# A graph layer on one core: the instruction order around the change from tiles to token pairs, written anew

## The reference, cut to what matters

```python
xn  = layernorm(x)
msg = (xn @ Wr[r])[src] * weight            # one 256x256 matrix for each kind of edge
x   = x + segment_sum(msg, dst)             # graph part
    + ((q @ softmax_over_nodes(k).T @ v) * sigmoid(gate)) @ Wproj + bproj     # mixer, 8 heads
x   = x + tokens + sum over the 2 chosen of 8 experts of weight * (gelu(t @ w1 + b1) @ w2 + b2)
```

## Time and profile before

| | us |
|---|---|
| median of 3 runs | 1622.17 (1618.7 to 1623.04) |
| profiled execution | 1618.12 |
| its span, first to last instruction | 1616.2 |
| PE busy in the span | 1565.0 (97%) |
| DVE, ACT, POOL busy | 1357.8, 964.5, 1012.3 |

### The profile page before, as it was taken

The page is one execution under the profiler, slowest core; times in us unless marked ns, Lnnn a source line. Parts: engine busy times, 40 slices in busy tenths (PEclk is TensorE's granted clock), DMA queues, the critical chain, the costliest instruction groups (busy, mean ns, idle before and its releaser), DMA issues.

```text
span 1616.2 us, 31822 instructions
## 1 busy us (share of the span) xinstructions
PE 1565.0 (97%) x10509; PEld 1439.1 (89%) x10509; DVE 1357.8 (84%) x3437; ACT 964.5 (60%) x2156; POOL 1012.3 (63%) x1115
## 2 busy tenths in 40 slices
PE   7999999799999999998599999999999999999998
PEld 6888888688888888887599999999999999999998
DVE  7888766398888888885789999999999999999985
ACT  4354322255655566553467777677767776777764
POOL 4534222677777777764567777777767677777730
PEclk9999999899999999999699999999999999999999
DMA  9776665588888888888433333334333333334320
GB/s 298 261 255 250 230 240 233 181 269 288 273 282 283 284 275 283 275 282 299 127 93 112 104 118 105 112 103 121 105 106 109 108 112 102 112 105 119 105 58 10
DMA packets 127078, 290.52 MB, mean 180 GB/s; under 512 B 21271, under 2 KB 49724, under 8 KB 126914
## 3 DMA queue, kind: packets, MB, share of 16 engines
q1 hardware_dynamic: 86068, 177.19, 30.1%
q0 software_dynamic: 39952, 110.13, 25.2%
q10 hardware_dynamic: 894, 1.16, 0.2%
HBM read 149.49 MB, written 138.90 MB: 178 GB/s over the span
## 4 chain that ended last, share of the span: by engine, by line
PE 84%; DVE 5%; issue 4%; DMA 2%; ACT 2%; POOL 2%; SPq 1%; DVEq 0%; ACTq 0%; POOLq 0%
PE bank L1870 67%; PE bank L2072 4%; PE bank L2073 3%; PE bank L1916 2%; PE bank L1917 2%; PE bank L1927 1%; DVE ml L1655 1%; DMA raw<-in_L_ffn_w 1%; PE bank L2110 1%; DMA xres<-in_L_gnn_weight 1%; PE bank L2122 1%; SPq L599 1%; DVE wreg L1223 1%; DVE pad L1290 1%; PE bank L1880 1%
## 5 line engine op out<-in xcount | busy, mean ns | idle before, releaser
L853 POOL DMA_INDIRECT stg<-table,idxcur x475 | 520.0, 1095 | 230.1 <-issue 148.6
L1870 PE MATMUL bank<-wreg,xt 128*128 128x512 f32 x2352 | 582.8, 398 | 1.3 <-DVE stg L1265 1.1
L1870 PEld LDWEIGHTS bank<-wreg,xt 128*128 128x128 f32 x2352 | 436.1, 190 | 89.8 <-DVE stg L1265 1.5
L732 POOL DMA_INDIRECT raw<-table,idxa x309 | 316.0, 1023 | 91.2 <-issue 80.8
L1870 PE MATMUL bank<-tt,wreg 128*128 128x256 f32 (+1 forms) x2400 | 320.4, 283 | 0.0
L1870 PE MATMUL bank<-wreg,ht 128*128 128x256 f32 x2352 | 313.8, 282 | 0.2 <-DVE ht L1771 0.2
L1870 PEld LDWEIGHTS bank<-tt,wreg 128*128 128x128 f32 x2400 | 297.5, 190 | 2.5
L1870 PEld LDWEIGHTS bank<-wreg,ht 128*128 128x128 f32 x2352 | 292.7, 189 | 0.4 <-DVE ht L1771 0.4
L1655 DVE SCALAR_TENSOR_TENSOR ml<-stg,nrm,mh 128x256 fp32r<-128x256 f32 x483 | 207.4, 478 | 26.8 <-ACT mh L1070 26.8
L1126 ACT ACTIVATE raw<-bank,cols 128x256 f32<-128x256 f32 (+1 forms) x400 | 164.9, 463 | 98.7 <-PE bank L1870 98.7
L1070 ACT ACTIVATE mh<-stg,nrm 128x256 fp32r<-128x256 f32 x483 | 213.1, 499 | 0.5 <-DMA stg<-table,idxa 0.5
(11 more groups left out here) (246 smaller groups left out, 2122.7 us busy)
## 6 DMA issues: line engine op xcount, KB each, us to landing
table<-stg SPq DMA_DIRECT2D x196, 512.0 KB, 3.7
kv_d<-kvs SPq DMA_DIRECT2D x49, 256.5 KB, 4.5
xt_d<-xt SPq DMA_DIRECT2D x49, 256.0 KB, 4.6
xtp<-xt_d SPq DMA_DIRECT2D x24, 512.0 KB, 3.8
stg<-table,idxcur POOLq DMA_INDIRECT x475
sk<-kv_d SPq DMA_DIRECT2D x24, 256.5 KB, 5.7
out_x<-xres SPq DMA_DIRECT2D x24, 256.0 KB
xres<-in_x POOLq DMA_DIRECT2D x23, 256.0 KB, 3.8
```

The lines of the kernel that those rows point to most:

```text
L732: pool.indirect_dma_start(ring_a[:, r * EARLY + j, :], None, table[0:limit, :], bass.IndirectOffsetOnAxis(ap=idxa[:, at:at + 1], axis=0)). ...
L853: pool.indirect_dma_start(stg[:, (g % 4) * SUP + j, :], None, table, bass.IndirectOffsetOnAxis(ap=where, axis=0)).then_inc(gath[g % 4], 16)
L1870: mm = pe.matmul(dst, stat(a, c), mov(b, c), start=(n == 0), stop=(n == 3 * chunks - 1))
```

## The change

The first early entry of tile 23 (entry 0) is prepared at the start of tile 23 on ACT and DVE and no longer within tile 22. At the change of phases `spot` maps the slots of i = 0 and i = 1 to other groups: slots 0 to 3 of i = 0 do pair 0's four groups, its slots 4 to 7 the first four groups of pair 1, and the first slots of i = 1 the other four. `SLOTS_OF_FIRST` and `SLOTS_OF_SECOND` name the new order. The weight splits, the turned context and the queries move to other places; `GATES` and `OUT` of pair 0 go behind the last group of i = 0; the table of the Gelu function is loaded in slot (0, 7) by a small activation; POOL's first `roots2` goes behind all gathers of pair 1; and ACT waits for the last weight split (`w_lo`, 8) directly behind `split_hi(7)`, ahead of `NORM`, where it waited in slot (1, 4) before.

```diff
+        def spot(i, s):
+            if i == 0:
+                return (0, 2 * s + 1) if s < 4 else (1, s - 4)
+            if i == 1:
+                return (1, s + 4) if s < 4 else None
+            return (i, s) if i < NP or i == NP and s < TAIL_GROUPS else None
...
# POOL
             gathers(0, 8)
             gathers(1, 8)
+            roots2(0, 2)
...
# ACT: tile_act and the change of phases
+                if at(k, K1):
+                    early_high(k, i, b, 0)
                 if 1 in rows:
                     early_high(k, i, b, 1)
...
-                if begin or rows and nxt:
+                if rows and nxt:
                     early_high(*nxt, 0)
                 table_out(k, 4)
...
+            def expert_high(n):
+                if n == 6:
                     act.wait_ge(ctx_mm, HELD + REST)
+                split_hi(n)
+                if n == 7:
                     act.wait_ge(w_lo, 8)
+            def gelu_table():
+                act.activation(small[0:1, 156:157], small[0:1, 157:158], ACT.Gelu).then_inc(table_kept, 1)
...
+                if (i, s) == (0, 5):
+                    expert_high(4)
+                if (i, s) == (0, 6):
+                    expert_high(5)
+                if (i, s) == (0, 7):
                     query_high()
+                    gelu_table()
                     GATE_ACT(0, 2)
...
# DVE: tile_dve as tile_act, with early_prepare; the change of phases
             def WINDOW(i, s, groups):
+                for at in range(max(8 * i + s - 2, 0), 8 * i + s):
+                    done = spot(at // 8, at % 8)
+                    if done and done[1] % 2:
+                        adds(done[0], done[1] // 2)
...
+                if (i, s) == (0, 5):
                     finish_context()
+                    turned_context()
+                if (i, s) == (0, 6):
                     head_contexts()
+                    split_lo(4)
                     dve.memset(halves(c3[:]), 0.0).then_inc(c3_clear, 1)
+                if (i, s) == (0, 7):
                     query_low()
+                    split_lo(5)
...
# PE
+                if (i, s) == (0, 5):
                     context_turn()
+                if (i, s) == (0, 6):
                     context_values()
+                if (i, s) == (0, 7):
                     query_context()
                     pe.wait_ge(xtp_in, 32)
                     GATES(0, 2)
                     OUT(0, 2)
...
+SLOTS_OF_FIRST = (
+    ("*SELECT", "*MSGS", "*SUMS"),
+    ("*SELECT", "*MSGS", "*SUMS"),
+    ("*SELECT", "*WINDOW", "*MSGS", "*SUMS"),
+    ("*SELECT", "*MSGS", "*SUMS"),
+    ("*SELECT", "*WINDOW", "*MSGS", "*SUMS"),
+    ("*SELECT", "*MSGS", "*SUMS"),
+    ("*SELECT", "*WINDOW", "*MSGS", "*SUMS"),
     ("*SELECT", "*MSGS", "*SUMS"),
 )
+SLOTS_OF_SECOND = (
+    ("+GATE", "+GATE_HI", "+GATE_LOW", "+PROJ", "+EXPERT_HI 6", "*WINDOW", "+EXPERT_LOW 6"),
+    ("+STATS", "*SELECT 0", "*MSGS 0", "*SUMS 0", "+EXPERT_HI 7"),
+    ("+MEAN", "+NORM", "+EXPERT_LOW 7", "+TURN", "+TURN_HI", "+TURN_LOW", "+LAYER1 0", "+LOGIT", "*SELECT 1", "*MSGS 1",
+     "*SUMS 1"),
+    ("+LOW 0", "*SELECT 2", "*WINDOW 2", "*MSGS 2", "*SUMS 2", "+TOP", "+LAYER1 1"),
+    ("*SELECT 3", "*MSGS 3", "*SUMS 3"),
+    (),
+    ("*WINDOW 4",),
+    (),
+)
```

More of the change, by code:

```diff
@@ L53, in gps_layer @@
     SUP = 4
-    ROOTS, FIRST_ROOTS = (7, 1), (5, 0)
+    ROOTS = (7, 1)
     EARLY = 3
@@ L1133, in slot_of @@
             def slot_of(i, s, groups, p1, n1, p2, n2):
[L1134 to L1138, removed]
+                if i + s == 0:
+                    for part in PARTS_OF_SLOT[0]:
+                        exps(part)
                 in_slot(i, s, groups, p1, n1, p2, n2, MSGS=MSGS, GATE_ACT=GATE_ACT, GATE_HI=GATE_HI, NORM=NORM,
-                        TURN_HI=TURN_HI, WEIGHT=WEIGHT, COMB_HI=COMB_HI, COMBT_ACT=COMBT_ACT, LAYER1=LAYER1)
-                if isinstance(i, int) and (i, s) == (0, 7):
+                        TURN_HI=TURN_HI, WEIGHT=WEIGHT, COMB_HI=COMB_HI, COMBT_ACT=COMBT_ACT, LAYER1=LAYER1,
+                        EXPERT_HI=lambda p, nt, n: expert_high(n))
+                if i == 0 and s > 0:
+                    for part in PARTS_OF_SLOT.get(s, ()):
+                        exps(part)
+                if (i, s) == (0, 5):
[3 more added lines that the diff above has]
+                if (i, s) == (0, 7):
                     query_high()
+                    gelu_table()
                     GATE_ACT(0, 2)
-                if isinstance(i, int) and i + s > 0:
-                    beside(i, s)
             run(slot_of, NP, TAIL_GROUPS)
@@ L1646, in MSGS @@
             def MSGS(i, s, groups):
-                if s >= groups or not live(i, s):
+                if not spot(i, s):
                     return
+                i, s = spot(i, s)
                 g = group_no(i, s)
@@ L2221 @@
     ("-ADD 3", "*SELECT", "-LOW 5", "*MSGS", "+MEAN", "*WINDOW", "-LAYER1 6", "+NORM", "-LAYER2 4"),
-    ("-ADD 4", "*SELECT", "-LOW 6", "*MSGS", "*LAST_WINDOW", "-LAYER1 7", "*SUMS 4", "+TURN", "+TURN_HI", "-LAYER2 5", "*SUMS",
+    ("-ADD 4", "*SELECT", "-LOW 6", "*MSGS", "-LAYER1 7", "*SUMS 4", "+TURN", "+TURN_HI", "-LAYER2 5", "*SUMS",
      "-BIAS2"),
@@ L2227 @@
 )
-SLOTS_OF_SECOND = (
-    ("*SELECT", "*MSGS", "*WINDOW", "+GATE", "+GATE_HI", "+GATE_LOW", "*SUMS"),
-    ("*SELECT", "*MSGS", "+PROJ", "*SUMS"),
-    ("*SELECT", "*MSGS", "*WINDOW", "+STATS", "*SUMS"),
-    ("*SELECT", "*MSGS", "+MEAN", "+NORM", "*SUMS"),
-    ("*SELECT", "*WINDOW", "+TURN", "+TURN_HI", "*MSGS", "+TURN_LOW", "*SUMS"),
-    ("*SELECT", "+LAYER1 0", "+LOGIT", "*MSGS", "*LAST_WINDOW", "+LOW 0", "*SUMS"),
-    ("*SELECT", "+TOP", "*MSGS", "*WINDOW", "+LAYER1 1", "*SUMS"),
+SLOTS_OF_FIRST = (
[6 more added lines that the diff above has]
+    ("*SELECT", "*WINDOW", "*MSGS", "*SUMS"),
     ("*SELECT", "*MSGS", "*SUMS"),
 )
+SLOTS_OF_SECOND = (
[9 more added lines that the diff above has]
+)
 def in_slot(i, s, groups, p1, n1, p2, n2, **steps):
-    for entry in (SLOTS_OF_SECOND if isinstance(i, int) and i == 1 else SLOTS_OF_PAIR)[s]:
+    for entry in {0: SLOTS_OF_FIRST, 1: SLOTS_OF_SECOND}.get(i, SLOTS_OF_PAIR)[s]:
         name, *expert = entry[1:].split()
```

65 lines of the change are left out of this document (19 added, 46 removed).

## The result

The changed kernel took 1627.84 us (median of 17 runs, 1623.49 to 1634.27), the kernel before 1622.0 (17 runs, 1617.46 to 1624.63): a ratio of 1.0043, 95% interval 1.0031 to 1.0054, which is 7.0 us, 5.0 to 8.8 (the medians lie 5.8 apart). It is slower, by about what the sum gave (+7.0).

The account below looks back on a forecast made before the run. PE was taken to bound the kernel except around tile 23 and at the change of phases; -0.5 and +7.5 us gave +7.0, predicted as 1629 us against a median of 1622.17, 8-in-10 range 1620 to 1633.

Parts of the forecast that it names:

- Part two: Change of phases, from finish_context to the third expert's first layer: the legs sum to +7.5 us.
- part one: Entry 0 inside tile 23: gain at the spot at most 3.1 us, not lasting; -0.5 us taken.
- to `query_context`: Leg from finish_context: 6.46 us before, 12.5 after (+6.0), as sums, messages and a split stand in the chain.
- to `STATS`: Leg from PROJ: 7.22 us before, 3.6 after (-3.6), as two groups' messages and a split leave the gap.
- to `NORM`: Leg from STATS: 3.58 us before, 6.3 after (+2.7), as ACT waits for the last split ahead of NORM.
- to the first layer: Leg from NORM: 5.37 us before, -1.6 after, as three messages and their hand-over no longer stand between.
- to the third: Leg from first layer: 13.75 us before, +2.1 after; Gelu table gone, but sums of (1, 6) and messages come ahead.
- to finish_context: Last context part behind the sums of group (1, 0), whose gather is used 4.6 us after issue: +1.2 us.
- Rival B: The gain at tile 23 lasts as gathers land sooner: PE keeps 3.1 us, +4.4 in all; chance 0.12.
- Rival A: PE's clock comes back at the change of phases, giving back 7.3 us: -0.3 us in all; chance 0.20.
- Rival C: Weights land late beside five more gathers, so NORM comes two to four us later: +10 us; chance 0.05.
- Rival D: The change does what it says: chain steps no longer wait for messages and splits, -5 us; chance 0.08.

Follow-up runs that it names:

- tile23_only: The kernel before with part one alone: entry 0 of tile 23 prepared at the start of tile 23; ratio to before 0.9992.
- phases_only: The changed kernel with entry 0 of tile 23 put back into tile 22, so the change of phases alone; ratio to before 1.0033.
- sums6_late: The changed kernel with the sums of (1, 6) behind the second layer instead of ahead of it; ratio to before 1.0013.
- chain_first: The changed kernel with the chain's context and query steps ahead of the groups' sums, messages and split; ratio to before 1.0010.
- three_moves: The changed kernel with chain steps ahead of groups' work, the last-split wait behind the turned rows, and sums of (1, 6) behind the second layer; ratio to before 0.9965.
- warm: The changed kernel with 149 products that nobody reads added ahead of PE's waits at the change of phases; ratio to before 0.9972.
- warm_three: The kernel three_moves with 118 products that nobody reads added ahead of PE's waits; 1611.04 us, ratio to before 0.9942.

## Why the prediction was right

- **Sign and size.** +7.0 us was forecast and 1.0043, 5.0 to 8.8 us, measured. Part two alone measured 5.4 (+7.5 in the sum), part one -1.3 (interval -3.4 to +1.0; -0.5 in the sum). That the size came out so close is in part luck: from the last early entry to the third layer the traces lose some 10 us in both pairs of profiles (84.9 before and 95.1 after, 83.7 in tile23_only and 94.1 in phases_only). The forecast missed 3.3 of these at `finish_context`, and the times show 3 to 4 less than the traces.
- **The legs behind finish_context**, forecast and in the trace after: to `query_context` 12.5 and 12.49; to `PROJ` +0.7 and +0.67; to `STATS` -3.6 and -3.95; to `NORM` +2.7 and +2.40; to the first layer -1.6 and -1.71; to the third +2.1 and +2.31. Their sum is +6.3 and +5.75. The largest three causes named for them were each undone alone and took the leg with them: the groups' work ahead of `query_context` (8.1 us of the leg, of which 3.2 came back up to `STATS`), the wait for the last split (2.2), the sums of (1, 6) (3.2 up to the second layer). That 12.5 was met to a hundredth is luck: the same steps took 11.3 in sums6_late, where the clock was at 1.00 from 776.4 to 786.6.
- **The term that was mis-sized: to finish_context**, +1.2 forecast, +4.5 in the trace. I took 4.6 us for a gather under the loads and full-speed context products. The gather took 6.46, at the upper end that the text named (2.3 late by that), and the last twelve products 4.55 instead of 2.7, mostly at half clock: 1.9 + 1.85 more than the 0.7 of the row of this stage. In the six profiles that keep the new order without added products the leg is 42.7 to 45.1; with them it is 40.4 and 40.6, no longer than before. But the clock of the last twelve products is only part of it. In chain_first and three_moves (these rows, in this order) they ran at the full clock, and the leg was still 43.1 and 42.7, 2.1 to 2.5 above before:

```profile
771.56 2.87 PE L2043 MATMUL bank<-later 128*128 128x257 f32 x12 [1.25 <-ACT later L1043]
```

```profile
769.17 2.87 PE L2046 MATMUL bank<-later 128*128 128x257 f32 x12 [1.25 <-ACT later L1043]
```

There the gather was used 5.7 and 5.9 us after its issue ended, in warm 5.0. No run separates the gather from the clock.

- **Part one.** The gain at the spot was 5.3 to 5.7 us, above the bound of 3.1. That bound took in the wait and the slow products at the third entry, but not what the same edit saved ahead of it: the second entry already came 1.6 to 2.0 us sooner, with the clock back at 1.00 from 315.2 in tile23_only, from 318.1 before. That it does not last held, and sooner than said: the last entry came 0.93 us sooner. Rival B fell by that trace; the interval of the times alone takes in its 3.1.
- **Rival A was under-priced.** The clock did not come back in the changed kernel, so the forecast stood. That the clock stayed low is no accident of the profile: over the whole span the granted clock has a median of 0.982 in the 17 runs of the changed kernel and of 0.986 in the 35 of the kernel before that were timed beside tile23_only. But rival A's result of -0.3 us left out the contexts: with the clock held, warm is 0.9972, some 4.5 us faster than before. The Trainium skill (TensorE: Matmul & The Clock Gate, section Part 1: The HAM clock gate) has a sustained busy stretch bring the full clock. By warm the trace agrees: with the waits filled the clock was at 0.96 over the stage. The same section puts the penalty of the ramp, which it describes for a kernel's first matmuls, below 1% of a typical kernel span; the 11.5 us here, at a change of phases, are 0.7%, and more than the change itself made.
- **Rival C**: ACT waited 0.20 us for the last chunk, at 799.21. The split that it fed ran on DVE only from 803.71, so nothing came of it in this kernel. **Rival D** fell with the leg of 12.49.

What stays open: the profiled executions before and after lie 16 us apart and the medians 6. 2.9 us of it lie ahead of the last early entry, where waits for gathers differ from one execution to the next: the same code took 7 us longer in the profile of phases_only than in that of before. 3.1 more lie behind the third layer, where the sums' high products lie 139 ns ahead of the product behind them after and 135 before (447 each, 2.2 us). That doesn't settle it: in phases_only they lie 121 ns ahead, and the stretch is still 2.2 us longer than before. The other 10 us are the stage itself. The profiled executions of the old order lie 3.9 and 2.5 us below the medians of their kernels (before, tile23_only), those of the new order 6.4 and 9.2 above (changed, phases_only), so these profiles overstate what an ordinary execution loses; where it loses less, no run shows.

## What to carry to other kernels

An order named for its chain is only as good as the queue in front of each step: read for every engine what stands between two steps of the chain, price it from rows of the same stage, and count splits and messages of other work as part of the leg. Where an engine's steps are short and lie between waits, ask what its clock does; products that nobody reads, sized to the waits, show in one run what the clock is worth, and here gave more than any single move to the changed kernel. Then read from the legs where they gave it: in warm_three the stretch that they were meant for came out as long as without them. Here most of a gain ahead of a stream that runs at the same pace (POOL's gathers) was gone within two tiles, so price a change where the pace is set.

## What the runs showed of the hardware

- 149 products that nobody reads made a kernel 11.5 us faster (1.0043 to 0.9972). The clock, at half from 778.7 to 812.9 and from 816.3 to 829.9 without them, was at half from 794.8 to 798.2 alone with them, behind PE's longest remaining wait there (2.51 us).
- The same form of gather took from its issue's end to its use 1.8 to 2.0 us at the first entries of tile 23 after the change, 5.5 at the seventh, and 6.46 beside the loads of keys, values and weights.
- The table load cost 1.28 us ahead of the gate in the changed kernel, as before at the first layer; the instruction ahead of it ended at 790.78 and it started at 790.80, and the next instruction started at 792.09, so no drain was seen beside it.
